# Attention: repeated query and key rows copied by VectorE, per two heads, in place of GpSimd

## What is computed

```python
scores = einsum('bhqd,bhkd->bhqk', q, k)
rel_q  = einsum('bhld,lrd->bhlr', q, pos_emb)      # pos_emb = dist_emb[l - r + M - 1]
rel_k  = einsum('bhrd,lrd->bhlr', k, pos_emb)
probs  = softmax((scores + rel_q + rel_k) / sqrt(D), axis=-1)
ctx    = einsum('bhqk,bhkd->bhqd', probs, v)
```

## Time and profile before

| | before |
|---|---|
| median of 3 runs | 3165.08 us |
| profiled execution, its own time | 3169.93 us |
| its span | 3168.1 us |
| busy over the whole span: PE, DVE, ACT, POOL | 84%, 64%, 51%, 56% |
| scores of the attention stage, first and last start | 1432.1 and 2526.2 us |
| copies on GpSimd (L886 and L890) | 64 of 1030 ns, 64 of 1034 ns |
| subtractions on GpSimd (L853) | 512 of 1563 ns |
| additions on VectorE (L1054) | 1024 of 686 ns |

### The profile page before, as it was taken

One profiled execution on the slowest core, in us unless ns is written; L12 is line 12 of the kernel. 1 busy time (PEld: TensorE's weight loads), 2 busy tenths in 40 slices (PEclk: granted clock), 3 DMA queues, 4 the chain that ended last, 5 costly groups with the idle time before them and its releaser, 6 DMA issues. The chain is left out here.

```text
span 3168.1 us, 51305 instructions
## 1 busy us (share of the span) xinstructions
PE 2673.8 (84%) x18316; PEld 1921.7 (61%) x18316; DVE 2019.4 (64%) x5579; ACT 1617.7 (51%) x2037; POOL 1785.3 (56%) x1486
## 2 busy tenths in 40 slices
PE   4676287978988888858999999999999959999998
PEld 2344187877877878755666666666666635554454
DVE  4665255655755666645666666666666658888885
ACT  2343164545544555526777777777777712222221
POOL 2333123333233233228888889988888825655555
PEclk7888667677776777768999999999999979999999
DMA  3999979999999999999999999999999532222110
GB/s 98 222 216 218 187 267 336 365 329 369 361 355 360 349 353 358 342 326 314 286 292 288 288 294 300 289 279 294 294 292 306 184 138 77 70 92 76 70 51 22
DMA packets 499917, 792.66 MB, mean 250 GB/s; under 512 B 236568, under 2 KB 266592, under 8 KB 465616
## 3 DMA queue, kind: packets, MB, share of 16 engines
q1 hardware_dynamic: 440528, 647.27, 61.4%
q10 hardware_dynamic: 46592, 100.68, 13.7%
q0 software_dynamic: 12544, 41.43, 4.5%
HBM read 449.17 MB, written 340.05 MB: 249 GB/s over the span
## 5 line engine op out<-in xcount | busy, mean ns | idle before, releaser
L1054 DVE CUSTOM_DVE_ANT_1 t_neg<-t_ps,t_r 128x512 f32<-128x512 f32 x1024 | 677.8, 686 | 355.2 <-issue 355.0
L733 DVE TENSOR_TENSOR d_r<-d_pq,d_r 128x1024 f32<-128x1024 f32 x512 | 620.7, 1224 | 436.0 <-PE d_pq L660 300.1
L853 POOL TENSOR_SCALAR t_neg<-t_neg,t_low 128x512 f32<-128x512 f32 x512 | 793.0, 1563 | 105.8 <-DVE t_low L1054 100.0
L708 ACT ACTIVATE d_r<-d_pk 128x1024 f32<-128x1024 f32 x512 | 519.4, 1028 | 518.0 <-PE d_pk L673 460.9
L975 PE MATMUL t_pt<-t_ident,t_neg 128*128 128x128 f32 x4096 | 627.5, 276 | 53.9 <-POOL t_neg L853 49.7
L1101 ACT ACTIVATE t_eT<-t_pt 128x1024 f32<-128x1024 f32 x512 | 524.6, 1025 | 258.3 <-PE t_pt L975 251.8
L975 PEld LDWEIGHTS t_pt<-t_ident,t_neg 128*128 128x128 f32 x4096 | 503.1, 142 | 178.2 <-POOL t_neg L853 86.0
L660 PE MATMUL d_pq<-d_win,d_q 96*128 96x128 bf16 x4096 | 502.5, 288 | 103.2 <-POOL d_q L612 76.2
L612 POOL COPY d_q<-d_q 32x4096 f32<-32x4096 f32 x64 | 236.1, 3689 | 602.2 <-DMA d_q<-q_chunks_scratch 602.2
L673 PE MATMUL d_pk<-d_win,d_k 96*128 96x128 bf16 x4096 | 478.5, 276 | 100.2 <-POOL d_k L612 59.2
L660 PEld LDWEIGHTS d_pq<-d_win,d_q 96*128 96x128 bf16 x4096 | 440.4, 189 | 135.7 <-POOL d_q L612 83.5
(11 more groups left out here) (145 smaller groups left out, 2525.0 us busy)
## 6 DMA issues: line engine op xcount, KB each, us to landing
r_scratch<-d_r SPq DMA_DIRECT2D x256, 1024.0 KB, 8.4
t_r<-r_scratch SPq DMA_DIRECT2D x1024, 256.0 KB, 7.9
d_q<-q_chunks_scratch ACTq DMA_DIRECT2D x64, 512.0 KB, 8.6
d_q<-q_chunks_scratch ACTq DMA_DIRECT2D x128, 256.0 KB, 11.6
q_chunks_scratch<-a_part SPq DMA_DIRECT2D x96, 128.0 KB, 3.8
q_rows_scratch<-a_part SPq DMA_DIRECT2D x96, 128.0 KB, 2.5
k_chunks_scratch<-a_part SPq DMA_DIRECT2D x96, 128.0 KB, 3.5
a_x<-in_x POOLq DMA_DIRECT2D x16, 512.0 KB, 5.6
```

Source lines behind the costliest of these rows:

```text
L708: nc.scalar.activation(r[lc % 2][:, :, n * KR:(n + 1) * KR], pk[n % 2][:].rearrange("p r l -> p l r"), ACT.Copy).then_inc(k_out, 1)
L733: nc.vector.tensor_tensor(part, pq[n % 2][:], part, ALU.add).then_inc(q_added, 1)
L853: nc.gpsimd.tensor_scalar(neg[:, j % RING, t, :], neg[:, j % RING, t, :], low[:, j % RING, t:t + 1], None, ALU.subtract).then_inc(pool_sub, 1)
L1054: nc.vector.tensor_tensor_reduce(out=neg[:, j % RING, t, :].rearrange("p (c r) -> p c r", r=TB), in0=p_s[t % 2][:].rearrange("p (c r) -> p ...
```

## The change

VectorE does the copies. A call moves two heads of either the queries or the keys, so a batch has 16 copies of half the size. They stand behind step 1's addition, one in each head, from head 10 of a batch to head 9 of the next; m counts them. The first six of the first batch stand ahead of VectorE's loop. The wait for the loads is taken once per batch, in the first of these copies. GpSimd's calls are gone, with its waits for its own copies.

```diff
-        COPIES = (10, 11, 12, 14)
+        CFIRST = 10
@@ gpsimd
-                def copy_rows(b, i, subtracted):
-                    heads = slice(b % 2 * H + GH * i, b % 2 * H + GH * (i + 1))
...
                 pool.wait_ge(ident_done, 1)
-                for i in range(BG):
-                    copy_rows(0, i, 0)
                 for n in range(NH + GH + 2):
                     head(n // U, n % U)
-                    b, j = n // H + 1, n % H
-                    if b < nb and j in COPIES:
-                        copy_rows(b, COPIES.index(j), 2 * (n + 1))
@@ tensor
-                pe.wait_ge(batch_copied, 2)
+                pe.wait_ge(batch_copied, 4)
...
-                                pe.wait_ge(batch_copied, 2 * (BG * b + (U * s + j) // GH + 2))
+                                pe.wait_ge(batch_copied, 4 * (BG * b + (U * s + j) // GH + 2))
@@ vector
+                def copy_rows(b, m):
+                    i = m // 4
+                    at = b % 2 * H + GH * i + GH // 2 * (m % 2)
+                    heads = slice(at, at + GH // 2)
+
+                    if m == 0:
+                        dve.wait_ge(batch_loaded, BATCH * (b + 1))
+                    if m // 2 % 2 == 0:
+                        nc.vector.tensor_copy(
+                            qa[T_Q_COPY:T_Q_COPY + T_PAIR, 0, heads, :].rearrange("r h w -> r (h w)").bitcast(F32),
+                            qa[0:T_PAIR, 0, heads, :].rearrange("r h w -> r (h w)").bitcast(F32)).then_inc(batch_copied, 1)
+                    else:
+                        nc.vector.tensor_copy(
+                            kb[T_K_COPY:T_K_COPY + T_PAIR, :, heads, :].rearrange("r c h w -> r c (h w)").bitcast(F32),
+                            kb[0:T_PAIR, :, heads, :].rearrange("r c h w -> r c (h w)").bitcast(F32)).then_inc(batch_copied, 1)
...
                         if not fixed or n < NH:
                             add(n, j, t, step)
+                        b, m = (n - CFIRST) // H + 1, (n - CFIRST) % H
+                        if t == 1 and b < nb:
+                            copy_rows(b, m)
...
+                for m in range(H - CFIRST):
+                    copy_rows(0, m)
                 rounds(dve, head, GH + 3)
```

## The result

The changed kernel is faster by about 1%, where I had forecast slower: 3131.99 us in the median of 4 runs (3130.82 to 3136.89), against 3165.14 us (4 runs). The ratio is 0.9895, with a 95% interval of 0.9868 to 0.9922, which leaves out 1. The profiled execution took 3131.82 us, its span 3130.0.

The account below looks back on a forecast made before the run. GpSimd, 89% busy in the attention stage, keeps TensorE waiting while VectorE idles. Removed copies -68, copy delays +116 and load waits +5 give +53 us: 3218 us, slower, range 3155 to 3275 (forecast's own 3190 to 3255).

Parts of the forecast that it names:

- Part 1: Attention stage: GpSimd's copies gone saves 4.24 us in each of 15 batches, plus 4 us at the start; 68 us removed.
- At the start: Before the first batch: six half-size VectorE copies replace eight GpSimd copies, so the first subtraction comes earlier; 4 us saved.
- Part 2: One VectorE copy of 32 x 512 f32 by itself takes 0.41 us, at 0.52 ns an element.
- Part 3: VectorE's copy waits 1.0 us for GpSimd's running subtraction to end, so the head's third addition starts 1.36 us later.
- The forecast's own signs of being wrong: Copies' mean under 0.7 us, a group of four heads under 16.6 us, or odd heads growing.
- Part 4: Per four heads, slack and V products cover some of the copy's delay; 1.86 us remain, +116 us in all.
- Slack of 0.13 and 0.43 us: Time the third addition can slip before delaying what follows: 0.13 us in a group's first head, 0.43 in its third.
- The second head's gain: Second head of four: -0.3 us, as the longer head before it ends TensorE's wait for GpSimd's late subtractions.
- GpSimd's backlog: GpSimd's subtractions need 3.10 us in a first head lasting 2.63, so TensorE waits for them in the second.
- Part 5: First copy of a batch: VectorE's wait for loaded rows is 0 in most batches; 5 us for 15 batches.
- a head 8 longer by 1.2 us: Head 8 of a batch takes 1.2 us longer, giving the loads more time before the batch's later copies.
- The rival that held: Attention stage: the copy does not wait for a subtraction; copies +9, loads +18, in all -41 us, 3124 us; chance 12%.

Follow-up runs that it names:

- copy_t0: Changed kernel with each head's copy behind step 0's addition instead of step 1's; 3171.76 us, ratio 1.0014 to the kernel before.
- sub_two_input: Changed kernel with GpSimd's subtraction as a two-input tensor_tensor instead of a tensor_scalar; 3161.45 us, ratio 0.9976 to the kernel before.
- odd_two_input: Changed kernel with four-head copies behind step 1 of odd heads only, from head 11, and GpSimd's subtraction as tensor_tensor; 3110.75 us, ratio 0.9811.
- first_copy_11: Changed kernel with all copies one head later, from head 11 of a batch instead of 10; 3113.22 us, ratio 0.9824 to the kernel before.
- copy_t3: Changed kernel with each head's copy behind step 3's addition instead of step 1's; 3141.64 us, ratio 0.9911 to the kernel before.
- copy_t2: Changed kernel with each head's copy behind step 2's addition instead of step 1's; 3150.11 us, ratio 0.9935 to the kernel before.

## Why the prediction was wrong

- **Part 1, what is removed: right.** 15 x 4.24 = 64 us forecast; a batch without copies is 4.22 us shorter. At the start 4 us were forecast, about 1.2 came: 0.6 until the first addition and 0.6 in the first batch.
- **Part 2, the copy by itself: right.** 0.41 forecast, 0.417 measured at 32 x 512. With 0.684 at 32 x 1024 the slope is 0.52 ns an element, as forecast.
- **Part 3, the copy beside GpSimd: this is the step that failed.** "So such an instruction waits until GpSimd's current one ends" was read from two-input operations of GpSimd and carried to a one-input subtraction. The wait of 1.0 us per copy was nought: 236 of the 256 copies started 0.54 to 0.62 us into a subtraction, when it lets a copy pass. The delay of a2 was 0.53 us, not 1.36. The forecast's own signs of being wrong came: the copies' median was under 0.7, and a group took 16.26, under 16.6. The Trainium skill, page "SBUF — State Buffer", section "Who interferes with whom", has the loser block for the whole instruction; with tensor_tensor on GpSimd the runs agree (copies end 0.28 us behind it), with tensor_scalar they don't (copies end 0.53 to 0.61 us ahead of its end). The same section says that issue order, not the shape of the operation, decides who blocks. copy_t0 agrees on the order: the copy was first, and the subtraction was held up. sub_two_input shows that GpSimd's operation matters too.
- **Part 4, what is covered: right in its rule.** Slack of 0.13 and 0.43 us with a delay of 0.53 gives +0.40 for the first head and +0.10 for the third; measured +0.45 and +0.05. The V products hid it in the other two. The second head's gain was -0.36 where I had -0.3, but that was luck: its cause was not GpSimd's backlog, which odd_two_input took away without effect, but by the traces ScalarE's. With the measured delay of 0.53 the sum of this part is +0.20 a group, and 0.14 was measured: +9 us, not +116.
- **Part 5, the loads: too small.** 5 us forecast, 1.49 x 15 = 22 measured (first_copy_11 and copy_t3 take it away). The forecast had let it vanish behind the wait for GpSimd, which wasn't there, and a head 8 longer by 1.2 us, which grew by 0.45.
- **The rival that held** was the first, 3124 us at 12%, with nearly the right terms (9 for the copies, 18 for the loads, where 9 and 22 were measured; its start of 4 us was 1.2). That a copy never waits for a subtraction is false all the same (copy_t2): the rival held by the place of the copies. Its chance was too low: the evidence against it was that of another operation, and I had said so and not priced it.

## What to carry to other kernels

An engine's wait that the trace shows for one operation is a fact of that pair of operations: before it is carried to another, price the case in which it isn't there as high as the case in which it is. What a copy costs on an engine with time to spare is decided by the place, from the slack of the step behind it: the same rows copied were 1.1% slower in lumps (the open wait for loads included), about 1% faster spread, and free in heads where other work stands in between. And where an engine is short of time, try its costly operation in another form first.

## What the runs showed of the hardware that I had not expected

- A tensor_scalar on GpSimd (128 x 512 f32, 1.56 us, the scalar a column of SBUF) lets VectorE's f32 copy pass in its middle. The places are those of GpSimd's recorded spans. A copy of 32 x 512 that starts in its first 0.5 us ends 0.96 us into it, that is, it starts to move at about 0.54; one of 32 x 1024, which takes 0.68, ends at 1.23. One that starts at 0.6 to 0.8 takes 0.42. One that starts later than about 1.0 ends 0.28 behind the subtraction, or more when it starts in its last 0.15 us. The last to pass started at 0.87 (copy_t3), the first to be held at 0.95 (copy_t2). When a copy of 32 x 512 ends 1.19 us in or later, the subtraction ends 0.47 behind the copy (recorded at 1.66 to 1.75). What the instruction does in its middle, no run shows.
- A tensor_tensor on GpSimd of the same size, with one input broadcast along the row, takes 1.04 us, two thirds of the tensor_scalar's time. It let none of the 246 copies pass that started 0.3 to 0.7 us into it.
- A copy that is first holds the subtraction up: 1.79 us in place of 1.57.
- The order of the two engines was the same in nearly every head: 247 of 256 copies in first_copy_11 started 0.55 to 0.60 us into the subtraction. Such a thing is no average. Moved by one addition, 178 copies were held at a subtraction's end (copy_t2, ratio 0.9935 in place of 0.9895).
